# A recurrent linear-attention and gated feed-forward layer on one core: two ternary products moved in the hand-written order of TensorE and ScalarE

## What is computed

```python
xn  = layernorm(x)
q, k, v = split(xn @ Wqkv + bqkv)
qp, kp  = elu(q) + 1, elu(k) + 1
kv, k_sum = kp.T @ v, sum(kp)                  # over the 2048 rows of a sequence
attn = (qp @ kv) / (qp @ k_sum + 1e-6)
z   = layernorm(xn + attn, g1, b1)
s   = layernorm(z + (silu(z @ Wg + bg) * (z @ Wu + bu)) @ Wd + bd, g2, b2)
g   = silu(xn @ (ternary(W).T * scale))        # ternary: each weight is -1, 0 or 1
out = x + s * g
```

## Time and profile before

| | |
|---|---|
| median of 3 runs (lowest, highest) | 1210.11 us (1208.1, 1210.26) |
| the profiled execution's own time | 1209.84 us |
| its span | 1208.1 us |
| granted clock of TensorE, mean | 0.998 of full speed |
| busy share PE, PEld, DVE, ACT, POOL | 98%, 88%, 89%, 79%, 70% |
| chain that ended last: PE, DVE, ACT, issue, DMA | 52%, 21%, 11%, 9%, 3% |

### The profile page before, as it was taken

How to read it: one execution, slowest core, us unless ns; L and a number is a source line. 1 busy time by engine, 2 the same in 40 slices (tenths; PEclk the granted TensorE clock), 3 DMA queues, 4 the chain that set the end, 5 groups by cost and what they waited for, 6 DMA issues and landing times.

```text
span 1208.1 us, 24021 instructions
## 1 busy us (share of the span) xinstructions
PE 1187.2 (98%) x7550; PEld 1067.3 (88%) x7550; DVE 1079.5 (89%) x2467; ACT 953.2 (79%) x1557; POOL 843.7 (70%) x994
## 2 busy tenths in 40 slices
PE   8999999999999999999999999999999999999997
PEld 6889998989988999988989989899988999888886
DVE  6988999999999999999999999999999999777765
ACT  7787888878888888888878888788887878867753
POOL 3443787767787776787757887677886767766676
PEclk9999999999999999999999999999999999999999
DMA  7213432334432334432334432244332343222201
GB/s 216 78 48 88 123 106 70 88 106 123 123 104 72 88 106 123 122 105 73 88 106 122 110 103 83 75 123 123 109 96 67 97 123 105 71 71 63 76 21 36
DMA packets 137523, 115.61 MB, mean 96 GB/s; under 512 B 12339, under 2 KB 122293, under 8 KB 137398
## 3 DMA queue, kind: packets, MB, share of 16 engines
q1 hardware_dynamic: 137398, 114.08, 32.6%
HBM read 67.38 MB, written 46.67 MB: 94 GB/s over the span
## 4 chain that ended last, share of the span: by engine, by line
PE 52%; DVE 21%; ACT 11%; issue 9%; DMA 3%; POOL 2%; SPq 1%; DVEq 0%; ACTq 0%; POOLq 0%
PE bank L1271 36%; PE d_bank L1271 11%; PE xk_bank L1271 5%; DVE st L922 3%; DVE bank L1095 3%; ACT rz L695 3%; DVE rz L1054 2%; DVE h_l L1105 2%; DMA xa<-z_turned 2%; DMA z_turned<-xa 2%; ACT h_h L695 1%; DVE zT_l L1085 1%; ACT ku L695 1%; POOL norm L569 1%; ACT hs L695 1%
## 5 line engine op out<-in xcount | busy, mean ns | idle before, releaser
L1271 PE MATMUL bank<-zT_h,wgu_h 128*128 128x512 f32 x704 | 275.1, 391 | 1.1 <-DVE rz L1054 1.1
L1271 PE MATMUL bank<-zT_l,wgu_h 128*128 128x512 f32 x704 | 275.1, 391 | 0.0
L1271 PE MATMUL bank<-zT_h,wgu_l 128*128 128x512 f32 x704 | 275.0, 391 | 0.0
L695 ACT ACTIVATE rz<-rz,norm 128x256 f32<-128x256 f32 x252 | 140.5, 595 | 53.6 <-DVE norm L1131 53.6
L569 POOL TENSOR_TENSOR norm<-ve,consts 128x4 f32<-128x4 f32 x64 | 72.9, 1139 | 154.7 <-DVE ve L933 154.5
L1271 PE MATMUL d_bank<-wd_h,h_h 128*128 128x256 f32 x640 | 179.4, 280 | 0.1
L1271 PE MATMUL d_bank<-wd_h,h_l 128*128 128x256 f32 x640 | 179.2, 280 | 0.0
L1271 PE MATMUL d_bank<-wd_l,h_h 128*128 128x256 f32 x640 | 179.2, 280 | 0.0
L1095 DVE SCALAR_TENSOR_TENSOR bank<-bank,hb,hs 128x512 f32<-128x512 f32 x160 | 117.9, 754 | 53.6 <-ACT hs L695 41.9
L695 ACT ACTIVATE h_h<-bank 128x512 fp32r<-128x512 f32 x160 | 95.7, 598 | 80.7 <-DVE bank L1095 80.4
L1271 PEld LDWEIGHTS bank<-zT_l,wgu_h 128*128 128x128 f32 x704 | 132.2, 188 | 28.1
(11 more groups left out here) (163 smaller groups left out, 3571.8 us busy)
## 6 DMA issues: line engine op xcount, KB each, us to landing
xq<-in_L_attn_x_dram SPq DMA_DIRECT2D x32, 512.0 KB, 5.9
xa<-in_L_attn_x_dram SPq DMA_DIRECT2D x31, 512.0 KB, 3.9
out_dram<-rz SPq DMA_DIRECT2D x31, 512.0 KB, 5.0
z_turned<-xa SPq DMA_DIRECT2D x120, 128.0 KB, 3.3
xa<-z_turned SPq DMA_DIRECT2D x30, 512.0 KB, 4.1
turned<-xa SPq DMA_DIRECT2D x108, 128.0 KB, 2.4
xa<-turned SPq DMA_DIRECT2D x27, 512.0 KB, 3.9
rz<-in_L_attn_Wg_dram SPq DMA_DIRECT2D x1, 640.0 KB, 5.7
```

The source lines that it names most:

```text
L695: return eng.activation(out_, in_, func, **kw).then_inc(S[name], 1)
L1271: ins = eng.matmul(dst, left, right, start=first and n == 0, stop=last and n == len(pairs) - 1, **kw)
```

## The change

In `TENSOR_JOBS` the job B 0 goes from ahead of U 2 to ahead of G 3, and B 1 from ahead of G 3 to a place between XK 1 and XK 2. In `SCALAR_STEPS` `silu_tern 0` goes from behind `h_high 1` to where `silu_tern 1` was, and `silu_tern 1` goes to a place behind `h_high 3`. `VECTOR_STEPS` and `GPSIMD_STEPS` hold the same steps in the same order, and so do the tables of the first and the last iterations.

```diff
 TENSOR_JOBS = steps("""
-    K 0, D 4, KV 0, KV 1, D 5, K 1, N 0, N 1, N 2, N 3, G 0, U 0, G 1, U 1, G 2, B 0, U 2, Q 0, Q 1,
-    B 1, G 3, D 0, D 1, U 3, G 4, XK 0, U 4, XK 1, XK 2, XK 3, GU 5, D 2, TZ 0, TZ 1, D 3""")
+    K 0, D 4, KV 0, KV 1, D 5, K 1, N 0, N 1, N 2, N 3, G 0, U 0, G 1, U 1, G 2, U 2, Q 0, Q 1,
+    B 0, G 3, D 0, D 1, U 3, G 4, XK 0, U 4, XK 1, B 1, XK 2, XK 3, GU 5, D 2, TZ 0, TZ 1, D 3""")
```

More of the change, by code:

```diff
@@ L90 @@
 TENSOR_JOBS = steps("""
-    K 0, D 4, KV 0, KV 1, D 5, K 1, N 0, N 1, N 2, N 3, G 0, U 0, G 1, U 1, G 2, B 0, U 2, Q 0, Q 1,
-    B 1, G 3, D 0, D 1, U 3, G 4, XK 0, U 4, XK 1, XK 2, XK 3, GU 5, D 2, TZ 0, TZ 1, D 3""")
+    K 0, D 4, KV 0, KV 1, D 5, K 1, N 0, N 1, N 2, N 3, G 0, U 0, G 1, U 1, G 2, U 2, Q 0, Q 1,
+    B 0, G 3, D 0, D 1, U 3, G 4, XK 0, U 4, XK 1, B 1, XK 2, XK 3, GU 5, D 2, TZ 0, TZ 1, D 3""")
 SCALAR_STEPS = steps("""
     xk_copy 0, zT_high 0, zT_high 1, x_res 0, x_res 1, kv_high 0, kv_high 1, x_res 2, x_res 3, k_exp 0,
[L95 to L98, removed]
+    last_rows 0, silu_gate 0, h_high 0, silu_gate 1, last_rows 1, h_high 1, last_rows 2, silu_gate 2,
+    last_rows 3, k_exp 1, k_high 0, q_exp 0, h_high 2, z_rows 0, z_rows 1, z_rows 2, z_rows 3, q_exp 1,
+    k_high 1, q_high 0, silu_tern 0, q_high 1, silu_gate 3, silu_gate 4, x_high 0, h_high 3, silu_tern
+    1, x_high 1, h_high 4, silu_gate 5, xn_high 0, xn_high 1, h_high 5""")
 VECTOR_STEPS = steps("""
@@ L102 @@
     h_low 0, h_rows 1, a_stats 0, h_low 1, q_aggregate 0, h_rows 2, a_norm 0, x_turn 0, attn_norm 0,
-    k_max 1, h_low 2, k_low 0, q_elu 0, z_turn 0, q_elu 1, q_low 0, k_low 1, h_rows 3, h_rows 4,
-    q_low 1, h_low 3, x_low 0, h_rows 5, x_low 1, h_low 4, h_low 5""")
+    k_max 1, h_low 2, k_low 0, q_elu 0, z_turn 0, q_elu 1, q_low 0, k_low 1, h_rows 3, h_rows 4, q_low
+    1, h_low 3, x_low 0, h_rows 5, x_low 1, h_low 4, h_low 5""")
 GPSIMD_STEPS = steps("""
```

## The result

| | before | after | 
|---|---|---|
| median of 12 runs (lowest, highest) | 1208.45 us (1207.0, 1210.66) | 1211.5 us (1209.81, 1213.82) |
| the profiled execution's own time | 1209.84 us | 1213.82 us |
| its span | 1208.1 us | 1212.1 us |

The ratio of after to before is 1.0024, with a 95% interval of 1.0015 to 1.0033: the change costs 2.9 us. The profiled execution of the changed kernel is the slowest of its twelve, so the two traces differ by more, 4.0 us.

The account below looks back on a forecast made before the run. The prediction took PE as the bound, held by a loop through GU 5, ACT and nearly gapless DVE work. It summed 3.9 - 1.1 + 1.9 = +4.7 us onto 1209.84, giving 1214.5 us, range 1208.0 to 1226.0.

Parts of the forecast that it names:

- The loop from GU 5 over DVE to U 3: GU 5 on PE, `silu_gate 5` on ACT, 25 us of gapless DVE work, then a DVE result PE waits for.
- the waits at Q 1: PE's waits for `h_low 1`, 4.6 us in all, were to go without lowering the sum, reappearing at U 3.
- U 3's wait, 0.14 us in 28 iterations: PE waits for `h_low 2` at U 3, 0.14 us in each of 28 iterations, 3.9 us in all.
- Its work stays the same: The tensor engine's work was taken as unchanged, so a new order could only add or remove waits.
- Half of it given back at `h_rows 5`, 1.1 us: The 0.07 us between `silu_gate 5` and `h_rows 5` on DVE give back about half of U 3's wait, 1.1 us.
- The disturbed iterations, 1.9 us: In 3 iterations `k_max 1` takes 1.30 us, and U 3 now pays 0.62 us each, 1.9 us.
- The base: The sum was added to the profiled execution's 1209.84 us, neglecting its 0.27 us below the then-known median of 1210.11.
- G 4 and the port, 0: PE's wait for `q_elu 0` at G 4 costs 0, not 0.57 us, as `k_low 0` goes ahead of POOL's `last_gate`.
- B 1's new waits, 0: B 1's wait for `silu_tern 0` and ACT's `x_high 0` waiting for B 1 were costed at nothing.
- Rival 2: B 1 is late for ACT: 28 x 0.1 to 0.2 us more, 1217 to 1220 us; chance 10%.
- Rival 3: Nothing gained or lost: DVE finds 0.1 us per iteration or disturbed `k_max` don't come, 1208 to 1212 us; 25%.
- Rival 4: Faster: Q 1's waits on `h_low` go and none replace them, at most 4.6 us, half gives 1207.5; 15%.

Follow-up runs that it names:

- experiment 1: Kernel before with only B 1 and `silu_tern 1` moved as in the change, B 0 left alone: 1206.95 us, ratio 0.9988.
- experiment 3: Changed kernel with D 1 moved from ahead of U 3 to behind it, so U 3 comes one job earlier: 1246.05 us.
- Experiment 7: Kernel before with GU 5 moved ahead of XK 2 and XK 3, nothing else: 1208.53 us, ratio 0.9994.
- experiment 5: Changed kernel with GU 5 ahead of XK 2 and XK 3 and, on ACT, `silu_tern 1` behind `silu_gate 5`: 1205.69 us, ratio 0.9972.
- experiment 9: Kernel before with B 1 then GU 5 between XK 1 and XK 2, and `silu_tern 1` behind `silu_gate 5`; B 0 stays: 1203.0 us, ratio 0.9953.
- experiment 4: Changed kernel with GU 5 moved ahead of XK 2 and XK 3: 1209.89 us, ratio 1.0008.
- experiment 12: Changed kernel measured again, unaltered: 1211.2 us, ratio 1.0016 against the kernel before.
- Experiment 11: Kernel before with B 1 and `silu_tern 1` alone moved as in the change, and D 2 ahead of GU 5: 1246.95 us.
- experiment 2: Kernel before with B 0 directly ahead of B 1 and `silu_tern 0` ahead of `silu_tern 1`; B 1 stays: 1333.72 us.

## Why the prediction was right or wrong

**The mechanism and the direction were right, the size was not.** The loop from GU 5 over DVE to U 3 is there. U 3 waits for `h_low 2` in quiet iterations too, a job goes on 0.19 us after what it waits for, and the waits at Q 1 went without a gain. Experiments 1 and 3 show that the loss hangs on U 3's wait for `h_low 2`: with another bank at a turn that is just as early it is gone, and with the turn a job earlier the period grows by that job. Experiment 7 fits: where U 3 doesn't wait, a shorter way from GU 5 gives nothing that can be told. A time of 1211.5 us is in the range; the forecast of 1214.5 was 3 us too high. It lies 6 us above the median of the kernel before, and 2.9 were measured.

**The step that failed** is the one from the quiet iteration to the whole run: "I take 0.14 us in each of the 28 iterations", plus three disturbed ones, with all else put at nothing and on a base of 1209.84 us. The 0.14 us were right for the period of a quiet iteration. But outside of that picture the kernel before loses time, most of it in waits, that the changed kernel doesn't lose: by the traces 0.6 us in each of iterations 5 and 16 and 1.8 us behind iteration 26, 3.0 us that had no term. And the base was 1.4 us above the median of the kernel before. How much of the 3.0 us belongs to that one execution and not to the kernel is open.

**What stands on each term of the sum:**

- *U 3's wait, 0.14 us in 28 iterations.* The wait is 0.40 us. "Its work stays the same" was wrong: the number of matmuls did, their pace did not, and PE comes to U 3 0.26 us earlier. In the sum this hardly counts, since the loop and not PE sets the period: the period grew by 0.14 us, 3.9 us in all, as this term had it.
- *Half of it given back at `h_rows 5`, 1.1 us.* It didn't come. The 0.07 us between the end of `silu_gate 5` and `h_rows 5` were no slack: `h_rows 5` stands 2.33 us behind the start of GU 5 before (539.97 - 537.64) and 543.33 - 541.02 = 2.31 after. It was set by GU 5 and ACT already, and now it waits openly, 27 times. The loop is closed there, and experiments 5 and 9 show that this place counts: with GU 5 early, ACT's shorter way to `silu_gate 5` was worth 4 and 3 us.
- *The disturbed iterations, 1.9 us.* The price was right, 0.64 us each against 0.62 at U 3. The number is not a constant of the kernel: four in the first trace (2.6 us), three in the second.
- *The end of the run.* It had no term, and it is the largest miss: 1.8 us come back behind iteration 26, of which 1.3 in iteration 29 with the kernel before's wait at U 0. I had read the quiet iteration and multiplied, and not looked at the last five. Two iterations of the kernel before with waits of their own, 5 and 16, give back 0.6 us each as well. By the traces: 3.9 + 2.6 - 1.2 - 1.8 = 3.5 us, of 4.0 in the spans. What is left has waits behind it as well: the changed kernel loses 0.5 us more in iteration 7 (0.35 us at N 0 for `kv_l`) and 0.6 and 0.3 more in iterations 10 and 25 (U 0), and the kernel before has its own 0.37 us at N 0 in iteration 15, where the disturbed `k_max 1` then costs only 0.1 more than a quiet iteration.
- *The base.* I put the sum on the profiled execution's 1209.84 us, by the three times known then. The median of twelve runs is 1208.45. That alone is 1.4 of the 3 us. It may be in part the same thing as the wait at U 0 of iteration 29, which makes that one execution slower; with one trace of the kernel before this can't be told.
- *G 4 and the port, 0.* Right, with its reason: `k_low 0` fell to 0.67 us.
- *B 1's new waits, 0.* Right: `x_high 0` came 0.03 us behind the end of the step ahead of it, and experiment 1, which has the same B 1, gained. Rival 2 is out.

**The rivals.** Rival 3 (1208 to 1212 us) has the measured time in it, but not its reason: neither did DVE find time, nor did the disturbed `k_max 1` stay away. Rival 4 (faster) needed U 3 not to wait. It is what experiment 1 became, where B 0 stays.

**What stays open.** Why PE has two paces for the same matmuls; which event decides whether `k_max 1` or POOL is first in a given iteration; and whether the one wait at U 0 of iteration 29, which experiment 7 also has and experiments 1, 4 and 12 don't, is lost by the shift or by chance. That the changed kernel has such waits in one trace and not in the other speaks for chance.

## What to carry to other kernels

Take a move apart by its pieces and price each against the loop that sets the period: here moving B 1 alone was worth 1.4 us, and moving B 0 as well cost some 4.5, and the good half with a shorter way to `silu_gate 5` gave 5.8. When an engine is both busy and waiting, its own pace says nothing of the period; measure the period from one job to the same job of the next iteration, and then go through all iterations, the last ones too, for those that differ from it. Work out which bank each job draws before a job is moved in a ring: here the bank, more than the place, decided which job waits. Where two engines meet within hundredths of a microsecond, count the meeting as a cost of its own in every forecast.

## What was not expected of the hardware

Matmuls of 256 columns start every 118 ns in some stretches and every 113 ns in others, at a granted clock of 1.00 in both, with the same operands: D 2 took 1.42 us before and 1.36 to 1.38 after. The quick stretches begin behind a job of 512 columns that is the first of its kind after a B job, and that job itself is slower, 1.39 us instead of 1.36. Experiment 11 moved the border by one job, as that rule says. But they don't always begin there: in the kernel before, D 0 and D 1 behind G 3 are quick in 13 of the iterations 1 to 26 and slow in the other 13, and in these G 3 takes 1.37 or 1.38 us. The cause was not found.

In experiment 2, behind a standstill of PE of 3.3 us, the granted clock was 0.50 for 5.3 us.
